# A graph kernel's last gathered tile moved from GpSimd to single-row DMAs of SyncE

## What is computed

```python
h = jnp.maximum(_layernorm(x, axis=-1), 0.0)
msg_in = concatenate([h[src], edge_attr_64], -1)        # 212500 x 320
agg = segment_sum(msg_in @ W_message, dst, 12500)
h2 = layer_norm(relu(agg) + h) * s1 + b1
out = x + layer_norm(h + mlp3_skip(h2)) * s2 + b2       # three 256x256 layers
```

## Time and profile before

| | us |
|---|---|
| median of three runs | 2189.6 |
| the profiled execution | 2189.61 |
| its span, from first to last instruction | 2187.8 |
| POOL busy | 1598.8 |
| PE busy | 1700.8 |
| DVE busy | 960.6 |
| ACT busy | 393.6 |

### The profile page before, as it was taken

How to read it: one execution, slowest core, us unless ns; L and a number is a source line. 1 busy time by engine, 2 the same in 40 slices (tenths; PEclk the granted TensorE clock), 3 DMA queues, 4 the chain that set the end, 5 groups by cost and what they waited for, 6 DMA issues and landing times.

```text
span 2187.8 us, 31761 instructions
## 1 busy us (share of the span) xinstructions
PE 1700.8 (78%) x6728; PEld 1142.8 (52%) x6729; DVE 960.6 (44%) x4123; ACT 393.6 (18%) x1185; POOL 1598.8 (73%) x1672
## 2 busy tenths in 40 slices
PE   0149987888888788888788788878878878878887
PEld 0137765555555455555555555545545555545555
DVE  8956544344343434344343434434343434333345
ACT  2942111111111111111111111111111111111112
POOL 7547777777777777777777777777777777777772
PEclk9779999989888989999899899999998998999988
DMA  9966655555555555555555555555555555555542
GB/s 326 328 211 178 174 160 156 149 159 161 147 160 146 156 154 158 151 159 161 149 156 152 153 155 159 158 151 154 153 158 151 159 148 160 151 159 148 157 136 57
DMA packets 360746, 356.47 MB, mean 163 GB/s; under 512 B 250048, under 2 KB 303360, under 8 KB 360704
## 3 DMA queue, kind: packets, MB, share of 16 engines
q0 software_dynamic: 79872, 218.21, 34.6%
q1 hardware_dynamic: 221504, 83.44, 14.6%
q10 hardware_dynamic: 59328, 54.36, 7.8%
HBM read 329.39 MB, written 26.48 MB: 163 GB/s over the span
## 4 chain that ended last, share of the span: by engine, by line
POOL 66%; issue 21%; PE 4%; ACT 3%; DMA 3%; DVE 2%; POOLq 0%; SPq 0%; DVEq 0%
POOL ring L344 66%; PE acc_banks L489 2%; ACT xs L619 2%; DMA ring<-h_table,src_all 2%; ACT ring L619 1%; DMA xs<-x 1%; PE agg_bank L394 0%; PE agg_bank L399 0%; DVE x_stats L859 0%; PE y_bank L382 0%; PE z_bank L382 0%; DMA h_table<-xs 0%; PE acc_banks L394 0%; PE acc_banks L497 0%; ACT x_std L611 0%
## 5 line engine op out<-in xcount | busy, mean ns | idle before, releaser
L344 POOL DMA_INDIRECT ring<-h_table,src_all x1600 | 1530.8, 957 | 527.6 <-issue 484.4
L489 PE MATMUL acc_banks<-ring,onehot 128*128 128x320 f32 x3328 | 1147.9, 494 | 419.8 <-DMA ring<-h_table,src_all 341.9
L489 PEld LDWEIGHTS acc_banks<-ring,onehot 128*128 128x128 f32 x3328 | 673.4, 213 | 847.3 <-issue 689.2
L956 DVE TENSOR_SCALAR onehot<-iota,dst_rel 128x128 f32<-128x128 f32 x1664 | 354.4, 300 | 1157.5 <-PE acc_banks L489 1122.7
L533 ACT ACTIVATE uT<-z_bank,fp 128x128 f32<-128x128 f32 x196 | 79.1, 453 | 963.2 <-PE z_bank L388 959.2
L394 PE MATMUL agg_bank<-wm,ST 128*128 128x256 f32 (+1 forms) x582 | 164.2, 403 | 0.0
L394 PEld LDWEIGHTS agg_bank<-wm,ST 128*128 128x128 f32 (+1 forms) x582 | 105.6, 194 | 55.2 <-issue 35.1
L399 PE MATMUL agg_bank<-wl,u 128*128 128x256 f32 x392 | 111.6, 407 | 0.0
L549 ACT ACTIVATE std<-mv,eps 128x2 f32<-128x2 f32 x97 | 28.7, 296 | 448.9 <-DVE mv L677 448.9
L539 ACT ACTIVATE r_bank<-y_bank,fp 128x128 f32<-128x128 f32 x196 | 58.7, 337 | 280.3 <-PE y_bank L382 280.3
L382 PEld LDWEIGHTS y_bank<-u,wl 128*128 128x128 f32 x784 | 102.9, 191 | 5.3 <-issue 0.3
(11 more groups left out here) (166 smaller groups left out, 1032.0 us busy)
## 6 DMA issues: line engine op xcount, KB each, us to landing
ring<-edges SPq DMA_DIRECT2D x208, 256.0 KB, 3.6
ring<-h_table,src_all POOLq DMA_INDIRECT x1600, 2.8
xs<-x SPq DMA_DIRECT2D x14, 896.0 KB, 10.0
h_table<-xs SPq DMA_DIRECT2D x14, 896.0 KB, 5.0
h_in<-h_table ACTq DMA_DIRECT2D x98, 128.0 KB, 2.4
visit_rows<-h_table ACTq DMA_DIRECT2D x98, 128.0 KB
visit_rows<-x ACTq DMA_DIRECT2D x98, 128.0 KB
out<-o ACTq DMA_DIRECT2D x93, 128.0 KB
```

The costliest lines, as they stand in the source:

```text
L344: nc.gpsimd.indirect_dma_start(out=ring[:, g % RG * G + j, 0:D], out_offset=None, in_=rows, in_offset=bass.IndirectOffsetOnAxis(ap=src_all ...
L489: return nc.tensor.matmul(acc_of(at), onehot[:, (k % OG) * G + j, :], ring[:, k * G + j, :], start=False, stop=True, skip_group_check=True)
L956: op = nc.vector.tensor_scalar(onehot[:, ((k + AHEAD) % OG) * G + j, :], iota[:, :], dst_rel[:, bass.ds((g + AHEAD) * G + j, 1)], None, AL ...
```

## The change

SP takes over the last tile (slot 63) of rounds 1 to 24. Before its loop it waits until all of h is stored, then reads the sender numbers of those 24 tiles (128 each) into one row of the now free `xs`, by 24 DMAs of 128 separate numbers, and waits for them. In each of the 24 rounds, behind the eight edge DMAs, it loads 32 row numbers at a time into registers, and issues 32 DMAs, each of one row of 1 KB from `h_table` at a register's address into one partition of slot 63; four times over, so 128 DMAs. The loop is made by a form that carries a prefetch hint for its jump back. The edges of the last round stand behind the loop. GpSimd gathers 63 tiles instead of 64 in rounds 1 to 24, and all 64 in round 25. PE waits for the four semaphores of the rows ahead of tile 63 (and so ahead of the visit, when group 7 has one).

```diff
+BY_ROW = 32
+        rows_flat = xs[0:1, 0:2, :, :].rearrange("p s b d -> p (s b d)")[:, 0:ROUNDS * P].bitcast(I32)
+        row_src = rows_flat.rearrange("a (i p) -> a i p", p=P)
+        row_src_in = sem("row_src_in")
+        rows_in = [sem(f"rows_in{c}") for c in range(P // BY_ROW)]
@@ SP
-            with nc.sync.Fori(1, ROUNDS) as i:
+            for s in range(XS):
+                sp.wait_ge(h_stored[s], 16 * len(range(s, NX, XS)))
+            for i in range(1, ROUNDS - 1):
+                sp.dma_start(row_src[:, i, :], src[0:1, :, i * RT + RT - 1], allow_slow_non_contiguous=True).then_inc(row_src_in, 16)
+            sp.wait_ge(row_src_in, 16 * (ROUNDS - 2))
+            row_regs = registers(nc.sync, BY_ROW)
+
+            def load_rows(i):
+                for c in range(P // BY_ROW):
+                    at = numbers(nc.sync, row_regs, rows_flat, i * P + c * BY_ROW, NB * P - 1)
+                    for q in range(BY_ROW):
+                        lane_at = c * BY_ROW + q
+                        sp.dma_start(ring[lane_at:lane_at + 1, RT - 1, 0:D], h_table[bass.ds(at[q], 1), :]
+                                     ).then_inc(rows_in[c], 16)
+
+            with nc.Fori(1, ROUNDS - 1, engines=[mybir.EngineType.SP], hint_back_edge=True) as i:
                 for k in range(RG):
                     load_edges(k, i, i * RG + k + 1)
+                load_rows(i)
+            for k in range(RG):
+                load_edges(k, ROUNDS - 1, (ROUNDS - 1) * RG + k + 1)
...
-            for s in range(XS):
-                sp.wait_ge(h_stored[s], 16 * len(range(s, NX, XS)))
@@ GpSimd
-            def gather(g, rows, semaphores):
-                for j in range(G):
+            def gather(g, rows, semaphores, count=G):
+                for j in range(count):
...
-                gather(g, h_table, landed(g))
+                gather(g, h_table, landed(g), G - 1 if g % RG == RG - 1 and g < NG - RG else G)
@@ TensorE
-                    if j % PT == 0 and not raw:
-                        pe.wait_ge(gathered[k * PAIRS + j // PT], (p * ROUNDS + i) * (16 * PT))
+                    rounds = p * ROUNDS + i
+                    slot = k * G + j
+                    if last_by == "raw":
+                        return
+                    if slot == RT - 1 and last_by == "SP":
+                        for c in range(P // BY_ROW):
+                            pe.wait_ge(rows_in[c], rounds * (16 * BY_ROW))
+                    elif slot // PT == RG * PAIRS - 1 and last_by == "SP":
+                        pe.wait_ge(gathered[slot // PT], rounds * (16 * (PT - 1)))
+                    elif slot // PT == RG * PAIRS - 1 and j % PT == 0:
+                        pe.wait_ge(gathered[slot // PT], rounds * (16 * PT) - (ROUNDS - 2) * 16)
+                    elif j % PT == 0:
+                        pe.wait_ge(gathered[slot // PT], rounds * (16 * PT))
```

More of the change, by code:

```diff
@@ L471, in _, with group @@
                 open_acc(a)
-            def group(p, i, k, raw):
+            def group(p, i, k, last_by):
                 g = i * RG + k
@@ L478, in group @@
                 pe.wait_ge(onehots, p * NG + g + 1)
-                if raw:
+                if last_by == "raw":
                     pe.wait_ge(raw_ready, k + 1)
                 def rows_of(j):
-                    if j % PT == 0 and not raw:
-                        pe.wait_ge(gathered[k * PAIRS + j // PT], (p * ROUNDS + i) * (16 * PT))
+                    rounds = p * ROUNDS + i
+                    slot = k * G + j
+                    if last_by == "raw":
+                        return
[8 more added lines that the diff above has]
+                        pe.wait_ge(gathered[slot // PT], rounds * (16 * PT))
                 def tile(j):
@@ L515, in _ @@
             for k in range(RG):
-                group(0, 0, k, True)
+                group(0, 0, k, "raw")
             with nc.Fori(1, ROUNDS - 1, engines=[mybir.EngineType.PE], hint_back_edge=True) as i:
                 for k in range(RG):
-                    group(0, i, k, False)
+                    group(0, i, k, "SP")
             for k in range(RG):
-                group(0, ROUNDS - 1, k, False)
+                group(0, ROUNDS - 1, k, "GpSimd")
             with nc.tensor.If(passes > 1):
@@ L526, in _ @@
                         for k in range(RG):
-                            group(p, i, k, False)
+                            group(p, i, k, "GpSimd")
                 nc.tensor.nop()
```

## The result

The changed kernel takes 2160.13 us (median of four runs, 2158.84 to 2162.28); the kernel before takes 2189.06 us beside it (2185.91 to 2190.01). The ratio is 0.9871, with a 95% interval of 0.9859 to 0.9883: it is faster by 28.9 us. The prediction said 2276 us and slower; its range of 2157 to 2400 holds the measured time only because it reached down to rival A. Rival A, that SP keeps up and POOL stays the bound, had said 2159.

A forecast was written before the change was run, and what follows sets the result against it. It took POOL's gathers as the bound and SP's queue as the next: terms (a) to (e) sum to 83.4 us a round against POOL's 79.4, giving 2276 us, 4% slower; the 8-in-10 range was 2157 to 2400.

The forecast's parts named there:

- rival A: SP keeps up, hidden under POOL, which stays the bound: faster, 2159 us; chance 0.26.
- (b): SP's row DMAs: 0.51 us each, of which 0.339 is the issue; 128 a round take 65.3 us.
- the 78.5 at which SP takes over: SP's round in us at which the span equals POOL's 2157.5; reached with a row DMA of 0.472 us.
- (c): SP's four loads of 32 row numbers a round: 2.9 us each with copies and address work, 11.6 us in all.
- Rival C: Every register of a load is its own trip: 8.9 us for 32, C 110.6, 2927 us; chance 0.04.
- The other seven edge DMAs cost nothing: SP's edge DMAs behind the rows take 7 x 0.55 = 3.9 us, hidden while rows land and PE visits.
- (a): SP's edge DMA of group 7, which opens the round after PE frees its slots: 0.55 us.
- (d): Landing of the last row of slot 63 after SP issues it: 2.1 us.
- (e): PE's work after the rows land: 0.47 of a visit in group 7, 3.3 us, and the last tile, 0.55 us.
- Rival D: SP's DMA queue backs up behind an edge DMA: about 0.9 us a round, 22 us in all; no chance of its own.
- The formula: Span is 272.4 + 24 C, C being SP's round; it equals the span before at C = 79.8.
- POOL's pauses: Sign that the forecast is right: POOL idle for `group_free` late in rounds; no size given.

The follow-up runs named there:

- floor: Changed kernel with SP's row DMAs and PE's waits for them left out, GpSimd still gathering 63 tiles; 2158.74 us against 2187.2 for the kernel before.
- experiments 4 and 5: Changed kernel, each row DMA split: 4 into 2, 4, 8, 16 pieces by chunk, 3700.4 us beside 2938.39; 5 into sixteen throughout, 2341.79 beside 2190.35.
- all_16_ways: Changed kernel with every row DMA split into sixteen pieces to sixteen partitions; 2341.79 us against 2190.35 for the kernel before, ratio 1.0693.
- no_hint: Changed kernel with SP's loop made without the prefetch hint for its jump back; 2162.4 us against 2189.98 for the kernel before, ratio 0.9873.
- plus16: Changed kernel with 16 further one-row DMAs a round into a spare place, 144 instead of 128; 2219.09 us against 2188.41 for the kernel before, ratio 1.014.

## Why the prediction was wrong, point by point

**What bounds the kernel, and what the change removes: right.** POOL's pace is 1.261 us a gather in both kernels, and taking 24 away moved the end by what they cost. The 2159.3 us that the prediction gave for "nothing else came late" was measured as 2158.74 in floor and 2160.13 in the changed kernel.

**The failed step is (b), the issue of a row DMA.** It assumed 0.339 us from ACT's DMAs, on the argument that "the DMA itself hardly shrinks with its size": 1024 pieces take 373 ns and 128 pieces 339. That was a line through two far points, and it was extended to one piece, where the price doesn't lie on it: 228 ns at one, 316 already at sixteen (experiments 4 and 5). The other parts of a row were right, 0.037 and 0.029, and 0.410 - 0.228 - 0.066 leaves 0.12 between instructions where 0.10 had stood. The lower bound, 0.43, was too high as well. In the sum the term is 128 x 0.410 = 52.5 us instead of 65.3, 12.8 less. With it alone set right the sum is 70.6 us, under the 78.5 at which SP takes over, and the sign is right. The row fell below 0.472 us, which the prediction had named as the point from which A decides. The prediction had also said for A that no DMA of 1 KB was in the trace and that its issue could be below 0.339; it gave A 0.26.

The Trainium skill (DMA: Bandwidth & Descriptors, Why a DMA increments its semaphore by 16 and not by 1) says that a DMA is divided over the largest number of engines, at most sixteen, that divides the slowest dimension of both its sides, and names a tile of 128 partitions as a case of sixteen. What that makes of one row in one partition the trace decides: SP's queue has 231104 packets in the changed kernel and 224960 in floor, two for each of the 3072 rows, so a row went in one piece. The prediction's "128 x 16 small pieces a round" were 128. The trace of all_16_ways has 461357 packets against 369197 in the changed kernel, 30 more for each row, two for each further piece.

**(c), the loads: right.** A load of 32 takes 2034 ns (2.1 predicted) and its four groups of copies about 0.6. Loads and gaps of a round are 61.51 + 3.43 - 52.5 = 12.4 us against 11.6. Rival C, with 8.9 us a load, is out.

**"The other seven edge DMAs cost nothing": wrong, and in the other direction.** They stand directly behind one another and behind the rows, and take 10.25 us with the eighth, not 8 x 0.55 = 4.4. With the 0.72 ahead of them that is 11.0 us, where the prediction had 0.55 + 2.1 + 3.3 + 0.55 = 6.5 for (a), (d) and (e) together. So in place of the chain from row to landing, visit and tile it is the queue itself that closes the round. In rounds 2 to 12, where PE still waited for SP's rows or had just stopped, SP stood for freed slots twice, 1.4 and 2.8 us; the rest of its 82.5 us lies before, or behind, where POOL sets the pace. Why an edge DMA is slow there is seen in the windows: the first is the stretch of the edge DMAs, the second that of the rows (columns as in the earlier trace rows; the last two are DMA share and GB/s).

```profile
475.92:489.60 13.68, 11.41 (x40) 7.65 (x41) 1.66 (x8) 1.13 (x3) 10.33 (x12) 0.74 1.10 242
...
413.69:475.20 61.51, 45.64 (x210) 33.70 (x208) 31.03 (x131) 9.50 (x31) 46.56 (x50) 0.90 0.49 141
```

I read a share of about 1 as DMA engines that are full, and 0.49 as not. The first two edge DMAs of that round still issue in 403 and 390 ns; the six behind them take 631 to 1764. The row DMAs aren't needed for it: in floor, which has none, four edge DMAs of round 1 stand directly behind one another, and the third and fourth take 1654 and 1607 ns. The window of those four:

```profile
156.80:161.70 4.90, 4.90 (x22) 3.50 (x20) 3.88 (x18) 1.07 (x3) 3.77 (x4) 1.00 0.97 252
```

That the issue waits for the queue to drain is my reading of these together; no run separated it from some limit of the queue by itself. Rival D had such a backlog, at 0.9 us a round; it is 5.9, from 4.4 to 10.25.

Together: 83.4 - 12.8 + 0.8 + 4.5 = 75.9 us, the round of SP that the timeline shows. The errors went against one another: the edge DMAs took back a third of what the rows saved.

**The formula was right to some 4 us.** The span as 272.4 + 24 C gives 2163.6, 2218.8 and 2341.2 us for the C of no_hint, plus16 and all_16_ways (78.8, 81.1, 86.2); measured are 2162.6, 2214.7 and 2338.1. The point where SP takes over, 78.5, fits too: the changed kernel lies below it and its chain is POOL's, no_hint lies 0.3 above it and its chain is SP's. It can also be seen from the end: in the three kernels that SP bounds, the span ends 83.1, 84.1 and 82.4 us after the last edge DMA of group 7, in the changed kernel and in floor 107.5 and 107.2 after it.

**The small ones.** The 24 DMAs of row numbers took 130.9 to 146.4 us and a wait of 8.9, and POOL did not stand for them, as said. The jump back costs 0.2 us with its hint, as said, but some 2.3 more without it, which the prediction had not weighed: it is most of the room under POOL. The 20 us of waiting for rows in each round, which was to show the forecast right, appeared in no_hint with the time of the rival. It did mean there that SP's queue is what the end hangs on, but nothing on how much time that costs. POOL's pauses, the prediction's other sign, don't show it either: 5.0 us in no_hint, and 23.8 us in plus16, whose span is 55.7 us longer than the changed kernel's. They miss what stands behind POOL's last gather, 75.0 us in plus16 and 40.3 in the changed kernel: in the last round of plus16 POOL is through long before PE. Two sums of the prediction are off by 2 us, and nothing hangs on them: C = 110.6 gives 2929 and not 2927, a row of 0.56 with loads of 3.3 gives 2467 and not 2465.

## What to carry to other kernels

Before an issue is priced by a row of the trace, compare the shape of that DMA with the new one, and take two rows that differ in the number of pieces near the one you need, not far from it; where many are issued, 0.1 us of the issue decides the sign. Work out the point where the bound changes, as here 0.472 us a row: if the assumed price is within its own uncertainty of it, the chances have to say so. When an engine gets close to the bound's pace, neither the waits for the new work (439.4 us in no_hint) nor the pauses of the old bound (5.0 us) tell how much time is at stake: look at which of the two the chain that ended last runs over, and hold the pace of the new one against the point where the bound changes.

## What the hardware showed that I had not expected

- The issue of a DMA of 1 KB from SP's queue: 228 ns in one piece, 237, 253, 277 and 316 ns in 2, 4, 8 and 16.
- Eight DMAs of 1024 pieces of 256 B back to back take 10.25 us of their queue with the DMA share at 1.10, and an issue 1.04 us in the median of the kernel, though the first two of the eight still take 0.40 and 0.39; with time between them they issue in 0.373 each.
- A load of 32 registers takes 2034 ns, 64 a register; of 12, 850.
- Without the hint for its jump back, the gap between the last and first DMA of SP's loop is 2.8 to 3.5 us; with it the gap is 0.73.
